# A four-layer graph attention network on one core: three-product matmuls in place of float32 ones in the masked layers, with part of the elementwise work on GpSimd

## The reference, cut to what matters

```python
h = jnp.maximum(_layernorm(x, axis=-1), 0.0); x = x + L0(h)   # 4 heads of 64, masked attention
h = jnp.maximum(_layernorm(x, axis=-1), 0.0); x = x + L1(h)   # MLP 512, full attention, MLP 256, masked attention
h = jnp.maximum(_layernorm(x, axis=-1), 0.0); x = x + L2(h)   # masked attention, own node always seen
h = jnp.maximum(_layernorm(x, axis=-1), 0.0); x = x + L3(h)   # masked attention
# each attention, for one graph:
Wh = h @ W; s_i = Wh @ a1; s_j = Wh @ a2
e = leaky_relu(s_i[:, None] + s_j[None, :])
att = softmax(where(mask, e, -inf), axis=-1)
out = att @ Wh                                                 # 512x512 by 512x256
```

## Time and profile before

| | us | share of the span |
|---|---|---|
| median of three runs | 2925.74 | |
| span of the profiled execution | 2924.5 | |
| PE (TensorE matmul) busy | 2864.4 | 98% |
| DVE (VectorE) busy | 2449.0 | 84% |
| ACT (ScalarE) busy | 2306.6 | 79% |
| POOL (GpSimd) busy | 209.0 | 7% |

### The profile page before, as it was taken

How to read it: one execution, slowest core, us unless ns; L and a number is a source line. 1 busy time by engine, 2 the same in 40 slices (tenths; PEclk the granted TensorE clock), 3 DMA queues, 4 the chain that set the end, 5 groups by cost and what they waited for, 6 DMA issues and landing times.

```text
span 2924.5 us, 66977 instructions
## 1 busy us (share of the span) xinstructions
PE 2864.4 (98%) x25624; PEld 2637.4 (90%) x25624; DVE 2449.0 (84%) x7049; ACT 2306.6 (79%) x6303; POOL 209.0 (7%) x410
## 2 busy tenths in 40 slices
PE   7999999999999999999999999999999999999998
PEld 7899999899999999999999999999999999999886
DVE  6788888888888888888888888888888888888866
ACT  6678778778778787788787788787787877887776
POOL 2000000000000000000000000000000000000000
PEclk9999999999999999999999999999999999999999
DMA  2000000000000000000000000000000000000000
GB/s 80 1 11 14 16 16 16 16 1 16 16 16 16 16 1 16 16 16 16 2 16 16 16 16 16 2 16 16 16 16 13 5 16 16 16 15 2 2 1 30
DMA packets 16799, 42.06 MB, mean 14 GB/s; under 512 B 5344, under 2 KB 7392, under 8 KB 16480
## 3 DMA queue, kind: packets, MB, share of 16 engines
q1 hardware_dynamic: 16480, 37.77, 3.7%
HBM read 20.99 MB, written 16.78 MB: 13 GB/s over the span
## 4 chain that ended last, share of the span: by engine, by line
PE 85%; ACT 9%; DVE 4%; issue 1%; POOL 0%; DMA 0%
PE bank L515 45%; PE bank L584 23%; PE bank L620 7%; PE bank L536 4%; PE bank L572 3%; ACT junk L1022 3%; ACT junk L1031 2%; PE bank L672 1%; DVE O L916 1%; ACT Z L1175 1%; PE bank L560 1%; PE bank L698 1%; ACT Z L1068 1%; DVE oTlo L920 1%; ACT hT2hi L1177 0%
## 5 line engine op out<-in xcount | busy, mean ns | idle before, releaser
L584 PE MATMUL bank<-hw,R 128*128 128x257 f32 x3072 | 707.8, 381 | 1.6 <-ACT hw L1083 1.0
L584 PEld LDWEIGHTS bank<-hw,R 128*128 128x128 f32 x3072 | 567.0, 191 | 74.7 <-issue 3.6
L793 DVE SCALAR_TENSOR_TENSOR R<-bank,E,mask_ne 128x512 f32<-128x512 f32 x640 | 448.9, 741 | 3.1 <-PE bank L572 0.7
L1248 POOL TENSOR_TENSOR rs<-ve,mhalf 128x4 f32<-128x4 f32 x128 | 140.6, 1099 | 2659.4 <-DVE ve L745 1655.8
L1045 ACT ACTIVATE Z<-x,nm,rs 128x256 f32<-128x256 f32 x512 | 276.6, 595 | 52.7 <-DVE x L1010 32.0
L515 PE MATMUL bank<-wfc_hi,oThi 128*128 128x256 f32 (+1 forms) x1024 | 303.3, 296 | 0.0
L515 PE MATMUL bank<-wfc_hi,oTlo 128*128 128x256 f32 (+1 forms) x1024 | 289.8, 283 | 0.0
L515 PE MATMUL bank<-wfc_lo,oThi 128*128 128x256 f32 (+1 forms) x1024 | 289.7, 283 | 0.0
L620 PE MATMUL bank<-hw,R 128*64 128x65 f32 x8192 | 268.3, 224 | 0.3 <-DVE R L793 0.3
L620 PEld LDWEIGHTS bank<-hw,R 128*64 128x64 f32 x8192 | 250.3, 138 | 20.1 <-issue 9.9
L1068 ACT COPY Z<-bank 128x258 f32<-128x258 f32 (+1 forms) x512 | 180.9, 371 | 42.6 <-PE bank L515 41.9
(11 more groups left out here) (262 smaller groups left out, 8351.0 us busy)
## 6 DMA issues: line engine op xcount, KB each, us to landing
x<-in_x_dram SPq DMA_DIRECT2D x32, 512.0 KB, 3.5
out_dram<-x SPq DMA_DIRECT2D x31, 512.0 KB, 2.6
R<-in_adj_dram SPq DMA_DIRECT2D x2, 512.0 KB, 5.6
Z<-in_L_gnn_mlp_w_dram SPq DMA_DIRECT2D x2, 512.0 KB, 5.4
O<-in_L_gnn_W_fc_dram SPq DMA_DIRECT2D x1, 1024.0 KB, 6.9
out_dram<-x SPq DMA_DIRECT2D x4, 128.0 KB, 2.4
R<-in_L_gnn_W_dram SPq DMA_DIRECT2D x1, 256.0 KB, 3.9
R<-in_L_gnn_W_hand_dram SPq DMA_DIRECT2D x1, 256.0 KB, 6.5
```

The lines of the kernel that those rows point to most:

```text
L584: ins = e.matmul(bk[:, 0:257], P[:, j, i * 128:(i + 1) * 128], hw[:, j, 0:257], start=(j == 0), stop=(j == NBLK - 1))
L793: e.scalar_tensor_tensor(P[:, t, :], bank_of(b, "row", p)[:, :], m["E"][:, 1, h, j:j + 1], mask[:, j, :], ALU.max, ALU.mult).then_inc(up(" ...
L1248: e.tensor_tensor(m["rs"][:, :], m["ve"][:, :], mhalf[:, :], ALU.pow).then_inc(up("rs", b))
```

## The change

In the masked layers `attend` now makes three products of rounded parts, as `mm3` does, 258 columns wide. The hi part of P is cast by ScalarE (`high_P`) into hT, which is free by then; the lo part is made by GpSimd (`low_P`) in place in R. The hi part of hw is what `scale` writes, now rounded; its lo part is one VectorE instruction a block (`low_hw`). Two small columns are split on GpSimd (`columns`).

In the diff `low_hw` runs on VectorE, `high_P` on ScalarE, and all from `center` on runs on GpSimd. Moved to GpSimd as well: the lo parts of the full attention's weights and of layer 1's second input; the minimum step of both elu functions (`min(exp, 1)`); the sums over all rows (`presum`, from the projected rows, so that `sums` is two matmuls instead of six); and the centring. Layers 0, 2 and 3 no longer normalize ahead of the projection: GpSimd forms max(x - mean, 0) (`center`), and the factor rs is applied where ScalarE reads the projection out of PSUM (`evacuate`). Layer 1 keeps `normalize`. With one head the scores take two instead of three VectorE instructions. `TURNS` is new for all engines, with every step of all 32 batches listed and no repeated cycle. Squares of layers 2 and 3 are written into `ends` instead of `hns`.

```diff
             def attend(a, l, p):
                 for i in range(NBLK):
                     w.wait_ge(*freed(b, f"att{a}b", i))
-                    bk = bank_of(b, f"att{a}b", i)
+                    out = bank_of(b, f"att{a}b", i)[:, 0:258]
+                    cols = slice(i * 128, (i + 1) * 128)
+                    w.wait_ge(*at("Pl", b, a, 1))
                     for j in range(NBLK):
-                        w.wait_ge(*at("hw", b, l - 2, j))
-                        w.wait_ge(*at("P", b, p, j))
-                        ins = e.matmul(bk[:, 0:257], P[:, j, i * 128:(i + 1) * 128], hw[:, j, 0:257],
-                                       start=(j == 0), stop=(j == NBLK - 1))
+                        w.wait_ge(*at("hwlo", b, a, j))
+                        w.wait_ge(*at("hw", b, a, 4 + j))
+                        e.matmul(out, Ph[s][j][:, cols], hwr[s][:, j, 0:258], start=(j == 0), stop=False)
+                        e.matmul(out, Ph[s][j][:, cols], hwl[s][:, j, :], start=False, stop=False)
...
+                    for j in range(NBLK):
+                        w.wait_ge(*at("Pl", b, a, 2 + j))
+                        ins = e.matmul(out, Rr[s][:, j, cols], hwr[s][:, j, 0:258], start=False, stop=(j == NBLK - 1))
...
+                e.matmul(bk[:, 0:256], ones[:, :], Zr[s][:, 1824:2080], start=True, stop=False)
+                e.matmul(bk[:, 0:256], ones[:, :], Zr[s][:, 1056:1312], start=False, stop=True).then_inc(up("S", b))
...
+            def low_hw(l):
+                w.wait_ge(*at("E", b, l, 2))
+                for n in range(NBLK):
+                    w.wait_ge(*at("hw", b, l - 2, n))
+                    e.scalar_tensor_tensor(hwl[s][:, n, 0:F], raw[s][:, n, 0:F], m["E"][:, 2, 0, n:n + 1],
+                                           f32(hwr[s][:, n, 0:F]), ALU.mult, ALU.subtract).then_inc(up("hwlo", b))
...
+            def high_P(a, p):
+                for j in range(NBLK):
+                    w.wait_ge(*at("P", b, p, j))
+                    e.copy(Ph[s][j], R[s][:, j, :]).then_inc(up("hw", b))
...
-                    e.copy(raw[s][:, i, 0:n], bank_of(b, f"h{l}", i)[:, 0:n]).then_inc(up("raw", b))
+                    src = bank_of(b, f"h{l}", i)[:, 0:n]
+                    if l == 2:
+                        e.copy(raw[s][:, i, 0:n], src).then_inc(up("raw", b))
+                    else:
+                        e.activation(raw[s][:, i, 0:n], src, ACT.Copy, scale=m["rs"][:, i:i + 1]).then_inc(up("raw", b))
...
+            def center(l):
+                w.wait_ge(*at("mn", b, SQ[l]))
+                for n in range(NBLK):
+                    e.tensor_scalar(hn[:, n, :], x[:, n, :], m["mn"][:, n:n + 1], 0.0, ALU.subtract,
+                                    ALU.max).then_inc(up("hn", b))
...
+            def low_P(a):
+                for j in range(NBLK):
+                    w.wait_ge(*at("hw", b, a, 4 + j))
+                    e.tensor_tensor(Rr[s][:, j, :], R[s][:, j, :], f32(Ph[s][j]), ALU.subtract).then_inc(up("Pl", b))
...
+            def presum(l, q):
...
+                e.tensor_tensor(two, raw[s][:, 0:2, 0:F], raw[s][:, 2:4, 0:F], ALU.add).then_inc(up("hq", b))
...
+                e.tensor_tensor(one, two[:, 0, :], two[:, 1, :], ALU.add).then_inc(up("hq", b))
...
+                e.tensor_copy(hi, one).then_inc(up("hq", b))
...
+                e.tensor_tensor(lo, one, f32(hi), ALU.subtract).then_inc(up("hq", b))
...
+            yield from center(0)
             yield from power(e, w, b, 1)
+            for j in range(NBLK):
+                w.wait_ge(*at("hB", b, 4 + j))
+                e.tensor_tensor(oT["lo"][:, j, :], R[s][:, j, :], f32(oT["hi"][:, j, :]),
+                                ALU.subtract).then_inc(up("Plo", b))
...
+            for q in range(8):
+                w.wait_ge(*at("ef", b, q, 1))
+                e.tensor_scalar(exf(q), exf(q), 1.0, None, ALU.min).then_inc(up("mf", b))
...
+            for k in range(2):
+                w.wait_ge(*at("o3", b, k, 1))
+                e.tensor_tensor(hT[s]["lo"][:, k, :], ends[s][:, k * 512:(k + 1) * 512], f32(hT[s]["hi"][:, k, :]),
+                                ALU.subtract).then_inc(up("o3lo", b))
...
+            yield from presum(2, 0)
+            yield from columns(2)
+            yield from low_P(0)
+            for i in range(NBLK):
+                w.wait_ge(*at("eh", b, i))
+                e.tensor_scalar(tB[:, i, :], tB[:, i, :], 1.0, None, ALU.min).then_inc(up("mh", b))
...
+            yield from center(2)
             yield from power(e, w, b, 2)
+            yield from columns(3)
+            yield from low_P(1)
...
+            yield from center(3)
             yield from power(e, w, b, 3)
...
+            yield from presum(4, 1)
+            yield from columns(4)
+            yield from low_P(2)
```

More of the change, by code:

```diff
@@ L120 @@
-        ("2165544313200"),
+        "00112233445566778899aabbccddeeffgghhiijjkkllmmnntoouppvqqrrsstuv"
     ),
 }
-FIRST, ENDS = 3, 4
 def in_turns(batch, turns, loading):
-    going, loads = {}, loading()
-    def go(b):
-        if 0 <= b < B:
-            if b not in going:
-                going[b] = batch(b)
-            next(going[b], None)
-    start, cycle, end = turns
-    for c in start:
-        if c == "w":
-            next(loads, None)
-        else:
-            go(int(c))
-    for t in range(FIRST, B - ENDS):
-        for c in cycle:
-            go(t - int(c))
-    for c in end:
-        go(B - 1 - int(c))
-    for left in [loads] + list(going.values()):
+    going, loads = [batch(b) for b in range(B)], loading()
@@ L147, in in_turns @@
+    for c in turns:
+        next(loads if c == "w" else going[int(c, 36)], None)
+    for left in [loads, *going]:
         for _ in left:
@@ L239, in build @@
         s_wl = [new_sem(f"wl{n}") for n in range(7)]
-        s_al = [new_sem(f"al{n}") for n in range(7)]
+        s_al = {n: new_sem(f"al{n}") for n in (0, 2, 4, 5, 6)}
         s_adj = [new_sem(f"adj{n}") for n in range(2)]
@@ L705, in tensor_batch @@
             yield from row(5, 2, 0)
+            yield from sums(0)
             yield from attend(0, 2, 5)
@@ L720, in tensor_batch @@
             w.wait_ge(s_wlo, K_BEFORE[7] - 2)
-            yield from sums(1, W3)
             yield from project(4, hT[s], W3, 0, [at("hTlo", b, 3, k) for k in range(2)])
@@ L724, in tensor_batch @@
             yield from row(7, 4, 0)
+            yield from sums(1)
             yield from attend(2, 4, 7)
-        SQ = {0: 0, 2: 1, 3: 2}
         def stats(e, w, b, n):
@@ L910, in vector_batch @@
                     yield from joined(q - 2)
-                yield from small(q)
             yield from joined(6)
@@ L925, in vector_batch @@
             yield
-            for k in range(2):
-                w.wait_ge(*at("o3hi", b, k))
-                e.tensor_tensor(hT[s]["lo"][:, k, :], ends[s][:, k * 512:(k + 1) * 512], f32(hT[s]["hi"][:, k, :]),
-                                ALU.subtract).then_inc(up("o3lo", b))
-                yield
-            yield from split_sums(0)
             yield from scores(2, 1)
             yield from weigh(5, 2, 0, "gt")
+            yield from low_hw(2)
             def first(i):
@@ L978, in vector_batch @@
             yield from weigh(6, 3, 0, "self")
+            yield from low_hw(3)
             def finish2(i):
@@ L1001, in vector_batch @@
             yield from weigh(7, 4, 0, "ne")
+            yield from low_hw(4)
             def finish3(i):
@@ L1188, in scalar_batch @@
             yield from scale(2)
+            yield from high_P(0, 5)
+            yield from sent(0)
             def second(i):
```

376 lines of the change are left out of this document (254 added, 122 removed), and 9 rows, old and new, of tables (ONCE, SHARED).

## The result

The changed kernel takes 3695.23 us (median of four runs, 3689.84 to 3696.52) against 2924.7 us for the kernel before in the same job: a ratio of 1.2628, 95% interval [1.261, 1.2646]. The forecast was 2848 us, the range ended at 3025. So the sign, the size and the range were wrong.

The account below looks back on a forecast made before the run. TensorE was taken to set the 88.65 us period. DVE's 72.0 + 12.5 = 84.5 us, level with PE's 84.15, over 0.98 gave 86.2 us; -2.45 us x 32 = -78 us, so 2848 us; range 2765 to 3025.

Parts of the forecast that it names:

- What bounds the kernel before: Whole kernel: TensorE, busy 98%, sets the pace; lightening it gains until DVE (12.9 us slack), ACT (17.4) or POOL (82.6) fills.
- PE, -4.5 us a batch: Masked layers' products and sums on TensorE: cheaper passes save 4.5 us a batch, allowing a period of 84.15 us.
- DVE alone, 72.0 us: VectorE's own work: 8.8 us a batch gone, 5.0 us of low_hw new, leaving 72.0 us before any blocking.
- ACT came to 74.7 for my 71.8: ScalarE: casts and scaled evacuations replace normalizing, net +0.6 us, so 71.8 us a batch; it doesn't bind.
- The exclusion, 12.5 us: Shared SBUF port: VectorE idles for a third of POOL's 37.5 us of streaming, 12.5 us a batch.
- POOL, 44 us: GpSimd's total work a batch, 44 us (40 to 51), with one-input steps taken at 0.45 us; it doesn't bind.
- With the 2% that the busiest engine leaves over now, 84.5/0.98 = 86.2 us: Period: VectorE's 84.5 us, level with TensorE's 84.15, divided by 0.98 gives 86.2 us.
- Latency, counted 0: Masked layers: P's path to its last product grows some 2 us three times a batch, covered by other work; 0.
- The power leaves the path: Ahead of the projection: centring waits only for the mean, so the power (1.1 us) and variance leave its path.
- Start and end: Ends of the span: 88 us outside the 32 periods, left as they are.
- DVE becomes the bound: Rival, 30%: VectorE meets the exclusion by chance and never idles otherwise; slower, 3053 us, or 2982 with cheaper one-input steps.
- Late weights: Rival, 11%: TensorE waits for P's lo part three times a batch, 5 us a batch; no change, 2925 to 2940.

Follow-up runs that it names:

- d4: Changed kernel with GpSimd's moved work on 32 columns from the fourth batch on and the order of steps planned anew: 2933.91 us.
- d5: d4 with three of four passes of the third product also left out from the fourth batch on: 2889.98 us.
- a2: Changed kernel, each moved GpSimd instruction replaced from the fourth batch on by a 128x4 power of about 1.04 us, holding no port: 3276.02 us.
- b3: Kernel before, with four extra 128x4 powers on GpSimd after each power step from the fourth batch on: 2952.32 us.
- b2: Kernel before, with nine extra 128x4 powers on GpSimd after each power step from the fourth batch on: 3150.37 us.
- a1: Changed kernel, order kept, with every moved GpSimd instruction on 32 columns only from the fourth batch on: 2981.96 us.
- b1: Kernel before, with eight extra 128x512 subtractions on GpSimd after each power step from the fourth batch on, read by nobody: 3558.96 us.
- c1: Kernel before with the sums over all rows formed on GpSimd, shorter score steps and a new order; attention stays float32: 2903.01 us.
- a3: Changed kernel with only the centring on 32 columns from the fourth batch on: 3460.45 us.
- d1: Changed kernel with all its instructions, only the order of steps written anew for the measured durations: 3386.33 us.

## Why the prediction was wrong, step by step

**What bounds the kernel before: right, but read too strongly.** PE was at 98%. Yet d4 and d5 show that at 95% little of what it is spared arrives. "A change that lightens PE gains until one of these is full" was the first wrong sentence.

**PE, -4.5 us a batch: a size somewhat off.** 2.6 measured in d4, where the clock is 0.99. In the changed kernel itself PE is busy 97.5 us, because it idles and its clock falls: same 26904 records as d4, 3128 against 2776 us busy, at a granted clock of 0.911 against 0.987. I had priced no clock at all.

**DVE alone, 72.0 us: too low by 2.0.** a2, without the port, shows 74.0 a period, counted as the period is. `low_hw` takes 0.53 us unblocked, not the 0.42 of L857 (12 x 0.11 = 1.3 us). The other 0.7 are the score steps: three of 0.16 us became two of 0.24 (L867 and L865 of a2), which saves nothing where four times 0.17 had been counted. ACT came to 74.7 for my 71.8 and bound nothing.

**The exclusion, 12.5 us: the size right, by luck.** After minus a2 is 86.7 - 74.0 = 12.7 us a period. The turn-taking held for GpSimd's two-input steps. But GpSimd streamed 57 us a batch instead of 37.5, so the share lost was 22%, not the third that I chose, and the 26 one-input steps, which I counted in, hardly block at all. Two errors cancelled: too little streaming, too high a share. Over half of the loss, 215 us in the run, is `low_hw` alone, which its dependencies put beside `low_P`; "as often as chance has it" was the wrong picture. DVE came to 86.7 for my 84.5. The danger that I had called the largest was sized well, and it still did not give the time.

**POOL, 44 us: wrong by the one-input price.** Taken 0.45 with an upper bound of 0.70; measured 1.20 (centring), 0.86 and 0.95 (minimum). The upper bound took it that one input can't be dearer than two, which no row showed: the two-input form takes 0.84 (L1390). The 512-column ones took 1.41 for 1.15. Sum 63.2.

**"With the 2% that the busiest engine leaves over now, 84.5/0.98 = 86.2 us": this step failed.** It takes the time as the largest busy sum over 0.98. The largest sum is 97.5 us, and even that is a result of the waiting; with GpSimd's work narrow and the clock at 0.99 (d4) it is 85.5. The period is 114. The 0.98 didn't carry over: there are four engines in one fixed order each, three batches in flight, and much of the work of each batch one after the other. Delay that fits into the gaps costs 0.05 us a us (b3), and past them 0.30 (b2).

**Latency, counted 0: this is the same failure, at its source.** I followed one new chain (`low_P` to the last product), and that one was covered: 3.3 us of waiting (7.8 at the weight loads). The others I took as moved work. The centring was four instructions of 0.54 on ScalarE; it became four of 1.20 on an engine that has 63 us of other work queued in order, and the transposes of a bank take them one by one, so the last of the four holds up TensorE. "The power leaves the path" was true and small beside it. a2 against a1 puts GpSimd's length at 10.5 us a period.

**Start and end: right.** 692.3 - 5 x 113.8 is 123 us, 573.7 - 5 x 88.8 was 130.

**The rivals.** "DVE becomes the bound" had the sign, with 2982 to 3053, but DVE is 75% busy and bounds nothing. "Late weights" had the mechanism, TensorE waiting in order, at the wrong place, and priced at 5 us a batch where 25 were lost. What no case held is a loss without any full engine: the length alone costs 10.5 us a period with the fullest engine at 90% (a2), and the port comes on top of it. The chances that I gave add up to 101%.

**What would have shown it beforehand.** The waits of the kernel before: ACT waited 127 us for DVE's scores, and nearly every other wait of PE, DVE and ACT was below 60, with PE at 98%. I now read such a picture as an order that is fitted closely, and not as room; no run here tests that reading. And the chain length was countable: 26 one-input and 24 two-input instructions of GpSimd lie in the paths of each batch. Those that replace a step elsewhere are, as measured, 0.57 to 0.73 us longer than it (0.86 for 0.29, 1.20 for 0.54, 1.41 for 0.68); the others, `low_P` and the sums above all, are new.

## What to carry to other kernels

When work moves to an idle engine in a pipeline with fixed orders, don't compare busy sums: list each moved instruction that someone waits for, with its length before and after and what is queued ahead of it, and expect the sum of these to show in the period once it passes the gaps. Price GpSimd's elementwise work twice: its own length, and, for its two-input steps, the VectorE steps that will run beside them. Ask which these are, as no one rate holds: 0.60 us of VectorE went for each 1.35 us in b1, 371 us for 992 us of two-input steps in the changed kernel, some 14 for 212 in c1. And plan the order anew for the measured durations before judging a change: that alone was worth 309 us here, and 19 us on the kernel before.

## What the hardware showed that I had not expected

- GpSimd's one-input step with a per-partition operand and two operations (centring, 128x256) takes 1.13 us at least and 1.20 on average, with one constant 0.84 at least and 0.86 to 0.95 on average. The two-input addition of the same width takes 0.72 at least and 0.84 on average, a cast 0.40 at least and 0.50 on average.
- What blocks is the two-input step of GpSimd. The one-input steps (803 us in the run, 25 a batch) hardly do: four `low_hw` took 1.80 us beside centring and 4.73 beside `low_P`, and 269 us less of centring left VectorE's busy time where it was (a3).
- A VectorE step with a single SBUF input can be blocked as well (L895 on `rowt`, 0.287 to 0.911 us in b1), against what the prediction says of such steps; one that reads a bank is not (`weigh`, 0.74 in all kernels).
- The loss through the clock: the passes behind a short wait start 0.215 us apart at the lower level, 0.12 at the higher. The mean granted clock was lower where PE waited more: 0.995 before, 0.977 in a1, 0.956 in a2, 0.911 after. It does not follow from the busy share alone: d1 and b1 are both at 87% and have 0.956 and 0.931.
